# A post-norm decoder layer on one core: another order of the tile loop, four sets of norm figures, and block maxima masked in PSUM

## What is computed

```python
x = _layernorm(x + _L0_attn_ref(x, ...))                  # 1: state model
x = _layernorm(x + _L0_xattn_ref(x, ctx_4096, ctx_4096))  # 2: autocorrelation
x = _layernorm(x + _L0_ffn_ref(x, weight, bias))          # 3: quantised product
```

```python
shared_exp = floor(log2(max |t| of a block of 32)) - 2
scale = exp2(shared_exp);  v = t / scale
e = clip(floor(log2(max(|v|, 2**-10))), 0, 2);  step = exp2(e - 1)
q = clip(round(|v| / step) * step, 0, 6) * sign(v);  out = q * scale
```

## Time and profile before

| | |
|---|---|
| median of three runs | 350.65 us |
| the profiled execution | 347.13 us |
| its span, first to last instruction | 345.0 us |
| state model (slots 0 to 7) | 0 to about 131 us |
| tile loop and last half state | about 131 to 345 us |
| TensorE busy | 282.1 us, 82% |
| vector engine (DVE) busy | 278.7 us, 81% |
| ScalarE (ACT) busy | 240.5 us, 70% |
| GpSimd (POOL) busy | 169.6 us, 49% |
| chain that ended last, by engine | DVE 40%, PE 21%, ACT 17%, issue 11%, POOL 9% |

### The profile page before, as it was taken

The page is one execution under the profiler, slowest core; times in us unless marked ns, Lnnn a source line. Parts: engine busy times, 40 slices in busy tenths (PEclk is TensorE's granted clock), DMA queues, the critical chain, the costliest instruction groups (busy, mean ns, idle before and its releaser), DMA issues.

```text
span 345.0 us, 4471 instructions
## 1 busy us (share of the span) xinstructions
PE 282.1 (82%) x1096; PEld 111.5 (32%) x1096; DVE 278.7 (81%) x915; ACT 240.5 (70%) x562; POOL 169.6 (49%) x204
## 2 busy tenths in 40 slices
PE   1684988989889886775999999999999998877533
PEld 1221322322223232313444443444443444422111
DVE  6978989889889883336699999999999999985710
ACT  6063689788888886547477887888777887664622
POOL 1000513203204204003338878898888898988682
PEclk9999899999999998689899999999999999998955
DMA  6999499400314003300000000000000000000002
GB/s 215 395 312 352 144 170 204 108 24 1 106 32 152 0 0 56 68 0 1 1 1 3 0 0 34 30 30 5 29 30 35 30 30 3 30 31 33 30 30 91
DMA packets 14416, 24.56 MB, mean 71 GB/s; under 512 B 2612, under 2 KB 3252, under 8 KB 14391
## 3 DMA queue, kind: packets, MB, share of 16 engines
q1 hardware_dynamic: 12310, 20.09, 17.6%
q0 software_dynamic: 2080, 4.19, 7.2%
HBM read 15.89 MB, written 4.19 MB: 58 GB/s over the span
## 4 chain that ended last, share of the span: by engine, by line
DVE 40%; PE 21%; ACT 17%; issue 11%; POOL 9%; DMA 1%; POOLq 0%; DVEq 0%; SPq 0%; ACTq 0%
ACT big L719 6%; DVE big L1116 4%; DVE X L1051 4%; DVE big L1128 4%; DVE qa L1026 3%; DVE m L1097 3%; DVE qa L1024 3%; ACT L722 3%; PE ps L537 2%; PE ps L515 2%; PE ps L460 2%; PE ps L424 2%; PE ps L452 2%; DVE ctxf L270 2%; ACT big L696 2%
## 5 line engine op out<-in xcount | busy, mean ns | idle before, releaser
L1051 DVE SCALAR_TENSOR_TENSOR X<-ps,X 128x512 f32<-128x512 f32 x48 | 31.9, 679 | 12.1 <-PE ps L505 7.9
L607 ACT ACTIVATE big<-X,lnv 128x512 f32<-128x512 f32 x48 | 34.2, 713 | 9.3 <-DVE X L1051 9.3
L775 POOL TENSOR_TENSOR big<-X,qs 128x512 f32<-128x512 f32 x20 | 21.0, 1050 | 38.6 <-DVE qs L1028 38.1
L374 PE MATMUL ps<-ctx_ring,consts 64*128 64x512 f32 (+1 forms) x96 | 34.8, 619 | 1.6 <-issue 0.8
L424 PEld LDWEIGHTS ps<-consts,big 96*128 96x128 f32 x256 | 30.4, 195 | 14.9 <-issue 10.6
L424 PE MATMUL ps<-consts,big 96*128 96x64 f32 x256 | 32.6, 282 | 2.1 <-ACT big L719 2.0
L1128 DVE TENSOR_TENSOR big<-ps,ctxf 128x512 f32<-128x512 f32 x48 | 30.7, 682 | 4.3 <-PE ps L452 2.7
L859 POOL TENSOR_TENSOR big<-big 128x512 f32<-128x512 f32 x16 | 20.3, 1271 | 10.6 <-DVE big L1116 10.4
L1116 DVE MATCH_REPLACE8 big<-w,big 128x64 f32<-128x64 f32 x128 | 25.0, 208 | 0.1
L635 ACT ACTIVATE X<-X,lnv 128x512 f32<-128x512 f32 x32 | 24.7, 806 | 0.6
L791 POOL TENSOR_TENSOR big<-big 128x512 f32<-128x512 f32 x4 | 5.8, 1445 | 38.4 <-DVE big L1158 27.7
(11 more groups left out here) (172 smaller groups left out, 682.6 us busy)
## 6 DMA issues: line engine op xcount, KB each, us to landing
big<-in_xT_dram SPq DMA_DIRECT2D x4, 1024.0 KB, 9.3
ctx_ring<-in_ctx_dram SPq DMA_DIRECT2D x16, 256.0 KB, 2.9
out_dram<-X SPq DMA_DIRECT2D x16, 256.0 KB, 2.0
X<-in_x_dram SPq DMA_DIRECT2D x2, 1536.0 KB, 13.0
X<-rows_sb POOLq DMA_DIRECT2D x1, 3072.0 KB, 21.5
X<-in_wq_dram SPq DMA_DIRECT2D x1, 1024.0 KB, 7.7
X<-in_x_dram SPq DMA_DIRECT2D x2, 512.0 KB, 3.8
X<-rows_sb POOLq DMA_DIRECT2D x1, 1024.0 KB, 8.0
```

The source lines that it names most:

```text
L374: mm(bank(LANE_BANK[lane]), mat((CY_0, CY_1, CY_C)[f])[half, :], ctx_ring[half, r * N:(r + 1) * N], start=True, stop=True).then_inc(s_cfor ...
L607: squared[k] = chain(a(JUNK[k], row(n), ACT.Square, bias=st[:, 0:1], scale=-float(V), accum_out=st[:, 2:3]))
L1051: stt(row(m), bank(b), 0.0, row(m), ALU.add, ALU.add, accum_out=st[:, 0:1]).then_inc(s_sum[k], 1)
```

## The change

It leaves the computation as it is and changes:

- **The order and the lags.** Each engine's loop has its parts in another order and at other lags: TensorE's from `projection(t)` to `feed_forward(t - 10)`, DVE's from `attended(t)` to `fed(t - 10)`, ScalarE's to `squares(2, t - 9)`, POOL counts its steps from its own first part to `finished(t - 7)`. DVE has 27 steps, TensorE and ScalarE 26, POOL 24, where each had 22. `rounding` follows `largest` directly; `out_even(t - 8)` is a step behind `out_rest(t - 7)`; `projection(t)` ends TensorE's step.
- **Slot 8** keeps of tile 0 only TensorE's `projection(0)`. The last state's second product, now `mixed(SLOTS)`, stands at the end of TensorE's step 2; DVE adds its bias in step 2 behind `attended(2)`; its norm is in TensorE's step 5, ScalarE's step 4 and DVE's step 6.
- **Norm figures.** `stats` takes one of four sets (`SETS`), so that `attended`, `crossed` and `fed` of tile n wait for tile n-4. ScalarE's squares of a tile wait for those of the tile before.
- **Scales.** For a tile the block maxima go to PSUM (the first 16 columns of bank 4), and DVE only masks the exponent, from there to SBUF; it is the scale times 4. POOL takes the inverse by an integer subtraction of the bits from 2^127's, a new instruction ahead of `scaled`. Clamp and rounding constants are a quarter of what they were. `out_rest(n)` gains a wait for `block_scales(n-1)`, `block_scales(n)` one for `crossed(n)`. For the weights the maxima stay in `qa`.

The diff, without the renaming of `squared` and `scaled_by` and with the hunks that only take out the early parts cut:

```diff
@@ -29,9 +29,8 @@
 NBLK = V // BLK
 TOP = 8
 NG = VC * 2
-LAG = 7
+SETS = 4
 WROW = PAIRS - VC
-TINY = 2.0 ** -100
 MAGIC = 1.5 * 2.0 ** 22
 EVEN = 96
 HEAD = 32
...
@@ -185,13 +184,14 @@
-        lnv = sb("lnv", [P, 3 * 2 * 8])
+        lnv = sb("lnv", [P, 3 * SETS * 8])
+        ends = sb("ends", [P, NBLK], I32)
...
@@ -268,6 +268,10 @@
+
+        def stats(k, n):
+
+            return lnv[:, (SETS * k + n % SETS) * 8:(SETS * k + n % SETS + 1) * 8]
...
@@ -464,9 +468,10 @@
                 if here(n):
                     pe.wait_ge(s_pw, 3 * n + 1)
                     if n == 0:
-                        pe.wait_ge(s_qe[0], VC)
+                        pe.wait_ge(s_rs1, SLOTS + 2)
                     if n >= 1:
                         pe.wait_ge(s_sum[1], n)
+                        pe.wait_ge(s_amax[1], n)
                     mm(bank(4), mat(OI_C), PW[0], start=True, stop=False, skip_group_check=True)
             def out_even(n):
...
@@ -506,10 +511,24 @@
+            def mixed(m):
+
+                o, l = 1 - m % 2, (m - 1) // 2
+                hs = hid_last if m == SLOTS else hid
+                for j in range(2):
...
+                                  hs[2 * j + g], start=False, stop=(j == 1), skip_group_check=True)
+                last.then_inc(s_mlp, 1)
...
@@ -538,45 +557,33 @@
                                XN[o][g * D:(g + 1) * D, :], start=True, stop=True).then_inc(s_hidmm, 1)
                 if first:
                     context_pair(2 * m + 1)
-                if early:
-                    query_forms(0)
-                    correlation(0)
-                    projection(1)
-                if second:
+                if second and not early:
                     if m == 1:
                         pe.wait_ge(s_w2c, 1)
-                    for j in range(2):
-                        pe.wait_ge(s_act, 4 * m - 2 + 2 * j)
-                        if j == 1 and m in (3, 5, 7):
-                            pe.wait_ge(s_idb, 1)
-                            transposes(0, l, bank(4))
-                        for g in range(2):
-                            last = mm(XC[o][g * D:(g + 1) * D, :], w2_all[:, (2 * l + j) * D:(2 * l + j + 1) * D],
-                                      hs[2 * j + g], start=False, stop=(j == 1), skip_group_check=True)
-                    last.then_inc(s_mlp, 1)
+                    mixed(m)
+
             for m in range(SLOTS + 1):
                 slot(m)
-            for t in range(1, PAIRS + LAG):
-                feed_forward(t - 7)
-                weights_to_time(t - 4)
-                if t >= 2:
-                    projection(t)
-                if t == 2:
-                    pe.wait_ge(s_rs1, SLOTS + 2)
+            for t in range(1, PAIRS + 11):
+                weights_to_time(t - 7)
+                out_even(t - 8)
+                weight_rest_forms(t - 7)
+                weight_forms(t - 7)
+                feed_forward(t - 10)
+                correlation(t - 5)
+                if t == 5:
                     transposes(0, VC, bank(4))
-                weight_rest_forms(t - 4)
-                weight_forms(t - 4)
-                if t >= 3:
-                    correlation(t - 2)
-                out_rest(t - 4)
-                if t >= 2:
-                    query_forms(t - 1)
-                if t == 1:
+                query_forms(t - 4)
+                if t == 5:
+                    pe.wait_ge(s_qe[0], VC)
                     pe.wait_ge(s_sq1, SLOTS + 2)
                     mm(bank(4), mat(MEAN), SQ_LAST, start=True, stop=True).then_inc(s_var1, 1)
-                quantized_to_channels(t - 6)
-                out_even(t - 4)
+                quantized_to_channels(t - 9)
+                out_rest(t - 7)
+                projection(t)
+                if t == 2:
+                    mixed(SLOTS)
         @block.scalar
...
+                    if n:
+                        chain.wait(squared[k, n - 1])
...
@@ -732,31 +732,30 @@
             for m in range(SLOTS + 1):
                 slot(m)
-            for t in range(1, PAIRS + LAG):
-                if t >= 2:
-                    normalise(0, t - 1)
-                probabilities(t - 3)
-                if t >= 3:
-                    corr_out(t - 2)
+            for t in range(PAIRS + 10):
                 squares(0, t)
-                squares(2, t - 7)
-                quantized_out(t - 6)
-                factors(0, t)
-                last_factors(t - 7)
-                if t == 1:
+                corr_out(t - 3)
+                if t == 3:
+                    weight_channels(VC - 1)
+                squares(2, t - 9)
+                if t == 2:
                     act.wait_ge(s_h, SLOTS + 2)
                     a(SQ_LAST, H[:, N:2 * N], ACT.Square).then_inc(s_sq1, 1)
+                quantized_out(t - 7)
+                factors(0, t - 1)
+                top_exponentials(t - 3)
+                weights_out(t - 4)
+                log_sum(t - 3)
+                normalise(0, t - 1)
+                last_factors(t - 9)
+                squares(1, t - 5)
+                factors(1, t - 5)
+                normalise(1, t - 5)
+                if t == 4:
                     act.wait_ge(s_var1, SLOTS + 2)
                     chain.then_wait(a(RS_LAST, bank(4), ACT.Ln, bias=eps[:, :]))
                     a(RS_LAST, RS_LAST, ACT.Exp, scale=-0.5).then_inc(s_rs1, 1)
-                top_exponentials(t - 2)
-                weights_out(t - 3)
-                squares(1, t - 4)
-                log_sum(t - 2)
-                factors(1, t - 4)
-                normalise(1, t - 4)
-                if t == 2:
-                    weight_channels(VC - 1)
+                probabilities(t - 3)
         @block.gpsimd
...
                 pool.wait_ge(s_amax[which], count)
+                top = qs[:, 2 * par * NBLK:(2 * par + 1) * NBLK]
+                inverse = qs[:, (2 * par + 1) * NBLK:(2 * par + 2) * NBLK]
+                chain.then_wait(g_.tensor_tensor(inverse.bitcast(I32), ends[:, :], top.bitcast(I32), ALU.subtract))
...
-                    chain.then_wait(g_.tensor_scalar(VB, VB, 6.0, -6.0, ALU.min, ALU.max))
+                    chain.then_wait(g_.tensor_scalar(VB, VB, 1.5, -1.5, ALU.min, ALU.max))
...
-            for t in range(1, PAIRS + LAG):
-                if here(t - 5):
-                    if t == 5:
+            def block_scaled(n):
+
+                if here(n):
+                    if n == 0:
                         pool.wait_ge(s_qd[0], VC)
-                    if t >= 6:
-                        pool.wait_ge(s_qd[1], t - 5)
-                    scaled(1, row(t - 5), (t - 5) % 2, t - 4)
-                chosen(t - 3)
-                top_differences(t - 2)
-                mark = clamped(t - 5)
-                differences(t - 2)
-                rounded_off(t - 5, mark)
+                    else:
+                        pool.wait_ge(s_qd[1], n)
+                    scaled(1, row(n), n % 2, n + 1)
+
+            for t in range(PAIRS + 8):
+                block_scaled(t - 3)
+                chosen(t - 1)
+                top_differences(t)
                 finished(t - 7)
+                mark = clamped(t - 3)
+                differences(t)
+                rounded_off(t - 3, mark)
         @block.vector
...
@@ -1019,18 +1026,15 @@
             def blocks(ap):
                 return ap.rearrange("p (b k) -> p b k", k=BLK)
-            def scales(which, src, par):
-                sc = qs[:, 2 * par * NBLK:(2 * par + 1) * NBLK]
-                do(v_.tensor_reduce(qa[:, :], blocks(src), AX_X, ALU.max,
-                                       apply_absolute_value=True))
-                do(ts(qa[:, :].bitcast(I32), qa[:, :].bitcast(I32), 0x7F800000, None, ALU.bitwise_and))
-                do(ts(sc, qa[:, :], TINY, 0.25, ALU.max, ALU.mult))
-                v_.reciprocal(qs[:, (2 * par + 1) * NBLK:(2 * par + 2) * NBLK], sc).then_inc(s_amax[which], 1)
+            def scales(which, src, par, most):
+                do(v_.tensor_reduce(most, blocks(src), AX_X, ALU.max, apply_absolute_value=True))
+                ts(qs[:, 2 * par * NBLK:(2 * par + 1) * NBLK].bitcast(I32), most.bitcast(I32), 0x7F800000, None,
+                   ALU.bitwise_and).then_inc(s_amax[which], 1)
             def magic(which, count):
                 dve.wait_ge(s_scaled[which], count)
                 do(ts(MB.bitcast(I32), VB.bitcast(I32), 0x7F800000, None, ALU.bitwise_and))
-                ts(MB, MB, 1.0, MAGIC, ALU.max, ALU.mult).then_inc(s_magic[which], 1)
+                ts(MB, MB, 0.25, MAGIC, ALU.max, ALU.mult).then_inc(s_magic[which], 1)
             def seqs(ap):
                 return ap.rearrange("p (s t) -> p s t", t=L)
...
@@ -1055,24 +1059,24 @@
                 if here(n):
                     dve.wait_ge(s_y, n + 1)
                     dve.wait_ge(s_xb if n < WROW else s_xblate, 16)
-                    if n >= 2:
-                        dve.wait_ge(s_ln[0], n - 1)
```

(30 more changed lines are left out.)

51 lines of the change are left out of this document (23 added, 28 removed).

## The result

The changed kernel takes 334.06 us (median of four runs, 332.94 to 335.48); the kernel before, run beside it, 350.15 (349.11 to 350.81). The ratio is 0.9545 (0.9492 to 0.9598). The forecast was 338.3 (331 to 347), so sign and range hold; the narrower 335 to 343, which was given a chance of 0.60, is missed by 0.9. The profiled execution of after took 335.48, with a span of 333.3.

A forecast was written before the change was run, and what follows sets the result against it. DVE bounds the kernel at 10.42 us a step; after the change TensorE would, at 9.95. Fill and steps to 304.4 plus drain 28.2 give span 332.6, 12.4 less than 345.0; 350.65 - 12.4 = 338.3 us, range 331 to 347.

The forecast's parts named there:

- TensorE is freer than I count: Rival on TensorE's loop: larger idle or hidden loads, step 9.6 us or less, 334 us in all; chance 0.13.
- The bound of the step: In the tile loop, TensorE replaces DVE as the longest engine, at 9.95 us a step while all parts run.
- DVE's step: In the loop, DVE falls from 10.42 to 9.55 us: mask 0.20, 0.40 added for rounding meeting POOL's chosen.
- DVE idle 0.4 a step: Sign expected in the loop's trace if the forecast held: DVE without work for 0.4 us each step.
- The rival by which the mask's output in SBUF would keep it held: DVE's mask still waits for the shared port, step 10.4, only fill and drain gain: 347 us; chance 0.02.
- POOL's step: In the loop, POOL gains a 0.28 us subtract and 0.25 of waiting between scaled and chosen: 9.7 us.
- the port takes TensorE's place: Rival: DVE's second rounding instruction loses the shared port to POOL, whose step becomes 10.65 us; 347 us; chance 0.17.
- The fill: Before the loop's full steps: last state's bias 4.1 us earlier, tile 0's transposes 2.6 earlier, with half-clock lengths.
- W(0): Start of tile 0's transposes on TensorE (the number is the tile); forecast at 160.5 us, 2.6 earlier than before.
- The rival of the paid lags: In the fill, every extra step of lag costs a round trip: tile 0's transposes at 187, 365 us; chance 0.08.
- The drain: From the start of tile 15's transposes to the end: 28.2 us, bounds 26 and 31, against 28.8 before.
- From span to time: At the final sum, the 12.4 us gained in span was subtracted from the earlier median, 350.65, giving 338.3.

The follow-up runs named there:

- e5: The changed kernel with each projection of the tile loop computed twice into the same bank; 342.19 us.
- e7: The changed kernel with DVE's fed(t - 9) between largest and rounding instead of fed(t - 10) at the head of the step; 334.45 us.
- e3: The changed kernel with the block maxima in SBUF, not PSUM, and without out_rest's wait for the mask; 336.16 us.
- e10: The changed kernel with a tile's last scaling on DVE instead of POOL, and fed(t - 9) ahead of the rounding; 334.53 us.
- e12: The changed kernel with the last scaling on DVE behind the crossed tile's residual, and added matmuls in TensorE's steps 16 to 23; 335.34 us.
- e4: The changed kernel with three sets of norm figures instead of four; 334.00 us.
- e8: The changed kernel with the last state's second product back in TensorE's slot 8 instead of the tile loop's third step; 336.39 us.
- e9: The kernel before, in its old order, with the new scales but the block maxima in SBUF; 344.14 us.

## Why the prediction was right, and where it was not

**The number.** The measured 334.06 is also what the rival *TensorE is freer than I count* gave (334), with a step of 9.6 or less. The step is 9.72, between that and my 9.95. By spans the rival's forecast is 328.3 (345.0 less 350.65 - 334) and mine 332.6, where 333.3 was measured. So the rival's time came out by chance, through the step from span to time, in the last paragraph of this section.

**The bound of the step.** Right. TensorE sets the steps as long as all parts run (e5: +0.85 a step for +0.85 of work), with 9.72, not 9.95. The mis-sized term is TensorE's own work in a step, 10.42 less an idle of 0.46 at its end, worked out from the step of about 0.22 between four transposes. The trace of before has a step in which TensorE waits for nothing, the one between these two rows:

```profile
191.72 0.60 PE L440 MATMUL ps<-consts,big 128*128 128x128 f32 x4
...
201.58 0.65 PE L440 MATMUL ps<-consts,big 128*128 128x128 f32 x4
```

It is 9.86 and could have been read instead. From 9.86 to 9.72 the same instructions gain 0.14 in the new order; why is not shown. 9.72 is the lower bound that I had named (9.7). Six steps: 1.4 us.

**DVE's step.** The mask at 0.17 was forecast as 0.20; the rounding at 0.82 (0.42 and 0.40) takes 0.69 to 1.47 in the loop, 0.85 to 1.37 for most tiles. That it is held by `chosen` was right; that it costs DVE 0.40 changed nothing (e7). The sign *DVE idle 0.4 a step* did not come: DVE is busy for 9.92 of 10 us, since a held instruction counts as busy. The rival by which the mask's output in SBUF would keep it held is refuted: 16 masks with the operand in PSUM took 0.175, four with the operand in SBUF 0.438, all with the output in SBUF.

**POOL's step.** The subtract at 0.22 (forecast 0.28) is right. The 0.25 of waiting between `scaled` and `chosen` that I put in is not there. In its place top_differences went from 0.31 to 0.47 and the last scaling from 0.77 to 0.96, beside DVE's rounding: 0.35 in all. (Before had one such case, at 295.07, beside the rounding's instruction at 294.53: 0.48.) 9.44 + 0.35 = 9.79 of the 9.87 that the last six tiles take, where 9.7 was forecast: 0.9 us for the six. The rival *the port takes TensorE's place* expected DVE's second rounding instruction to lose the port to these two and POOL's step to be 10.65. In the loop it is the other way: DVE's L1037 keeps 0.43 for thirteen tiles, and POOL's instructions are longer. But for the last three tiles L1037 takes 0.89, 0.80 and 0.80, beside the last scaling: there the rival's mechanism is at work. The Trainium skill (SBUF — State Buffer, "Who interferes with whom") has the pair of ports locked for a whole instruction by whichever engine issues first; the trace agrees in direction, both ways: L1036 waits for the end of `chosen`, and the two POOL instructions that start beside L1036 and L1037 are longer by 0.16 and 0.19, though by less than the 0.32 for which each overlaps with DVE's (232.03 to 232.35, and 232.50 to 232.82), and in the drain L1036 took 0.43 though POOL's L885 had started 0.04 ahead of it (311.52 and 311.48). I had used the rule in one direction only.

**POOL comes into play at tile 10**, as forecast, but by another way than the missing projection alone: from the first tile that it finishes (212.75) on, POOL lost 0.16 a step (9.88 against 9.71), drawing on the slack that it had, and had used it up when TensorE's step became shorter. e3, e5 and e7 have the same 9.85 from there, whatever happened before. Relieving POOL in e10 brought nothing, because the edit made a ring of 9.88; e12, without the ring, gains 0.1 a step while DVE is full and more in the last two.

**The fill.** Forecast W(0) 2.6 earlier, measured 5.9. Up to H's bias the argument held and the wrong step is the clock: I took half-clock lengths (3.68, 1.71, 1.8) from before. L524 took 1.94 and not 3.68 (1.7 of the 3.3), and the two projections about 1.1 and 1.0 and not 1.71 and 1.8 (1.4). L556, 1.99 and not 2.65, brings nothing in this sum, since it starts 0.66 later than before. Behind H's bias the same 3.3 is luck: largest(0) starts 6.5 behind the bias and not 7.5, and from its end to W(0) it is 7.7 and not 6.9. The forecast had the softmax and `chosen` set W(0); in this execution `chosen` ended 1.1 ahead of it and TensorE's queue, at half clock again, set it. In e4, where the clock stayed, `chosen` did (156.04, after a wait of 0.45). After the same 1.95 of idle, of eleven kernels with the new order nine show 1.99 for L556 (in e5 after 1.08 of idle), one 2.54, one 3.02; the three with the old order 2.65, 3.28 and 2.48. L524 takes 1.94 in ten of the eleven (2.23 in e8, whose order is the old one there). Why L556 itself, with the same idle in front of it, differs is not settled.

**The rival of the paid lags** decided at W(0) = 174.7; W(0) was 157.19. It is out. e8 shows how close fill and clock hang together: 2.2 us of product ahead of tile 0 put W(0) 2.9 later than in after, 0.4 of which is a later end of the state model.

**The drain.** 32.1 instead of 28.2, the one place where it got worse than before. (Not all of this repeats: e4, whose drain has the same instructions, takes 30.5 from W(15), and 41.0 from W(14), where after takes 41.9.) Written as a sum: POOL takes up tile 14 at W + 8.9 (310.14), each of the last two tiles keeps POOL for 7.2 (310.14 to 317.38 to 324.6), and product, norm and store take 8.7: 32.1. Forecast were W + 6.3, twice 6.4 with a gap, and 8.8. The first term is the clock: from its transposes the forms of tile 15 take 6.6 us until L507 (301.22 to 307.80) and 3.66 in the loop (232.38 to 236.04). I had let tile 15 run at the full clock, as before, though my own sum had TensorE waiting for POOL in those steps. The second is POOL's chain with DVE's rounding in the middle: 311.50 to 312.87. POOL has its last scaling L885 there (311.48 to 312.51), which takes 1.03, not 0.77, and L1037 beside it takes 0.80, not 0.43; POOL then waits 0.36 for L1037, for each of the last two tiles. In e12, where nothing of POOL stands beside it, L1037's counterpart takes 0.43 (310.55).

**"The four figure sets only remove waits", "the higher lag itself costs nothing at the end"**: e4 says of the first that the fourth set is not needed, and no run has two. Of the second no run is a test by itself; that both terms above have other causes speaks for it.

**From span to time.** Of the 4.2 us by which 338.3 missed, 3.5 come from one sentence: I carried the difference between the profiled execution of before (347.13) and its median (350.65) over to after. In the later runs the kernel before stood at 347.9 to 348.3 in four places. The difference was one of executions, not of the kernel: after's profiled execution is 1.4 above its median, which is most of the rest. 347.13 - 12.4 = 334.7 would have been the forecast against the profiled run, which took 335.48.

## What to carry to other kernels

A new wait between engines has to be followed through the order in which it will stand: the new scales cost 3 us in one order and brought 10 in the other. When several engines are within 2% of the bound, relieving one (POOL by 0.96 in e10, DVE by 0.23 in e7) can bring nothing, and where the edit has made a ring, only the sum of the ring across its engines shows why. Where TensorE's waits will grow, look for rows at half clock in a trace with such waits: here 0.8 us of waiting a step (tiles 10 to 13) left the clock full, and behind waits of 2.25 and 1.25 it was half. And anything put into the last steps, even to keep the clock up, belongs behind the last tile's work.

## What the runs showed of the hardware

- A 16-wide mask on DVE with its source in PSUM takes 0.17 or 0.18 in all 16 tiles of after, POOL busy beside it or not; with its source in SBUF it takes 0.44 (the weights of after), 0.45 (e3) and 0.93 (e9) on average.
- The two engines stretch each other: POOL's 128x64 tensor_tensor 0.31 to 0.47 and 128x512 tensor_scalar 0.77 to 0.96 beside DVE's tensor_scalar from SBUF to SBUF. Where the residual (a PSUM source) runs beside it, top_differences is back at 0.29 (the step shown of e10; 0.32 on average there). When both start within 0.04 us of each other, in the drain, the pair of 0.43 and 0.43 on DVE takes 1.26 in all and the 0.77 on POOL 1.03.
- The granted clock after the same 1.95 us of idle was the full level in some kernels and half in others, and within one kernel it fell behind waits of 1.26, 2.25 and 1.25 us (291.36, 298.67 and 301.22 of after). In e4 it was half already at 290.10, after a wait of 1.25, where after, with 1.26 at 291.36, was still full.
- An integer subtract of 128x16 on POOL takes 0.22, about as much as its smallest other instruction (128x8 fp32, 0.21).
